# Attention and FFN in two layers on one core: the splitting of the row maxima moves from VectorE to GpSimd, and two projections change places

## What is computed

```python
# layer 0
x = x + attention(tc_rmsnorm(x, t, g1w, g1b, b1w, b1b), Wq, Wk, Wv, Wo)
y = x + (silu(h @ gate_w.T) * (h @ hid_w.T)) @ out_w.T      # h = tc_rmsnorm(x, ...)
# layer 1
attn = softmax(where(mask, -inf, q @ k.T * D ** -0.5))
out = (attn @ v) @ Wo.T
xn = out / sqrt(mean(out * out) + EPS) * rms_scale * (1 + sc) + shift
```

## Time and profile before

| what | value |
|---|---|
| median of 3 runs | 1013.13 us (1012.89 to 1013.67) |
| the profiled execution | 1013.52 us, its span 1011.7 us |
| mean granted TensorE clock | 0.955 |
| busy: PE, DVE, ACT, POOL | 91%, 66%, 51%, 36% of the span |

### The profile page before, as it was taken

One profiled execution on the slowest core, in us unless ns is written; L12 is line 12 of the kernel. 1 busy time (PEld: TensorE's weight loads), 2 busy tenths in 40 slices (PEclk: granted clock), 3 DMA queues, 4 the chain that ended last, 5 costly groups with the idle time before them and its releaser, 6 DMA issues.

```text
span 1011.7 us, 24345 instructions
## 1 busy us (share of the span) xinstructions
PE 916.5 (91%) x8188; PEld 784.3 (78%) x8188; DVE 663.7 (66%) x1424; ACT 515.9 (51%) x1066; POOL 361.8 (36%) x376
## 2 busy tenths in 40 slices
PE   3568899999999999999999999999998888988884
PEld 2446698898888988988889889989886767767663
DVE  3476658667576686675765766656567777878751
ACT  2235546546455455364454554554456655656452
POOL 5322334334343434333334343333433333434221
PEclk9769999999999999999999999999999999999885
DMA  5554422432242233222422242333346575766700
GB/s 177 135 105 106 105 64 60 83 72 56 50 98 48 62 70 76 63 58 58 94 42 63 70 89 65 76 68 73 82 97 147 138 166 134 161 145 147 159 23 23
DMA packets 83070, 91.29 MB, mean 90 GB/s; under 512 B 7776, under 2 KB 70016, under 8 KB 83008
## 3 DMA queue, kind: packets, MB, share of 16 engines
q1 hardware_dynamic: 83008, 90.50, 40.1%
HBM read 60.30 MB, written 29.36 MB: 89 GB/s over the span
## 4 chain that ended last, share of the span: by engine, by line
PE 63%; DVE 16%; issue 7%; DMA 6%; ACT 4%; SPq 2%; POOL 1%; DVEq 0%; ACTq 0%; POOLq 0%
PE work L515 10%; PE work L517 10%; PE work L516 10%; PE s2ps L596 6%; DMA stack<-rows 5%; PE pvps L612 5%; PE s1ps L573 5%; PE work L699 3%; PE work L646 3%; DVE nmax L871 2%; PE acc L515 2%; PE acc L516 2%; PE acc L517 2%; DVE th L967 2%; DVE nrest L889 2%
## 5 line engine op out<-in xcount | busy, mean ns | idle before, releaser
L1067 ACT ACTIVATE E<-s2ps 128x512 f32<-128x512 f32 x384 | 214.0, 596 | 196.6 <-PE s2ps L596 123.7
L871 DVE TENSOR_REDUCE nmax<-s1ps 128x2 f32<-128x512 f32 x256 | 163.9, 682 | 15.8 <-PE s1ps L573 15.1
L515 PE MATMUL work<-xch,Gh 128*128 128x256 f32 x512 | 154.4, 302 | 0.1
L1305 POOL TENSOR_TENSOR hl<-hf,hh 128x256 fp32r<-128x256 f32 x128 | 94.7, 740 | 148.2 <-PE acc L517 93.1
L516 PE MATMUL work<-xcl,Gh 128*128 128x256 f32 x512 | 147.2, 287 | 0.0
L517 PE MATMUL work<-xch,Gl 128*128 128x256 f32 x512 | 147.1, 287 | 0.0
L967 DVE SCALAR_TENSOR_TENSOR th<-th,work 128x256 f32<-128x256 f32 x128 | 53.9, 421 | 136.6 <-ACT th L1085 135.4
L596 PE MATMUL s2ps<-stack 100*128 100x256 bf16 x768 | 128.8, 277 | 9.7 <-DMA stack<-rows 9.4
L515 PEld LDWEIGHTS work<-xch,Gh 128*128 128x128 f32 x512 | 99.5, 194 | 8.4 <-issue 6.6
L612 PE MATMUL pvps<-E,vaug 128*32 128x256 f32 x1536 | 98.7, 391 | 5.9 <-ACT E L1067 3.6
L517 PEld LDWEIGHTS work<-xch,Gl 128*128 128x128 f32 x512 | 100.0, 195 | 0.0
(11 more groups left out here) (130 smaller groups left out, 2192.3 us busy)
## 6 DMA issues: line engine op xcount, KB each, us to landing
stack<-scr SPq DMA_DIRECT2D x64, 384.0 KB, 4.7
stack<-scr SPq DMA_DIRECT2D x64, 256.0 KB, 5.4
scr<-qp SPq DMA_DIRECT2D x64, 192.0 KB, 2.3
scr<-kp SPq DMA_DIRECT2D x64, 192.0 KB, 2.3
stack<-scr SPq DMA_DIRECT2D x64, 128.0 KB, 5.7
X<-xT SPq DMA_DIRECT2D x16, 256.0 KB, 4.7
yT<-crm SPq DMA_DIRECT2D x16, 256.0 KB, 5.5
stack<-rows SPq DMA_DIRECT2D x196, 4.0 KB
```

Source lines behind the costliest of these rows:

```text
L515: mm(out, lh, rh, start=first, stop=False, skip_group_check=True)
L871: v.tensor_reduce(nmax[:, g // 4, qh, 2 * (g % 4):2 * (g % 4) + 2], s1ps[u % 2][:, :].rearrange("p (h t) -> p h t", h=2), AX_X, ALU.max, n ...
L1067: a.activation(E[:, exp_slot(st.L["B2"], st.full, g, kh), :], s2ps[g % 2 if short else u % 2][:, :], ACT.Exp, scale=SCORE_SCALE).then_inc( ...
L1305: p.tensor_tensor(hl[:, i % 2, :], hf[:, i % 2, :], hh[:, i % 2, :].bitcast(F32), ALU.subtract).then_inc(h_low, 1)
```

## The change

GpSimd takes the four small operations of `shift_split`; DVE keeps the clamp, which now stands in slots 3 and 7. There are no copies among them: where DVE cast, GpSimd multiplies by ones. The transposes of the parts come later: half 1 in slot 1 instead of 0, half 0 from step 19 on in slot 5 behind the scores instead of slot 4, with ACT's copy in slot 6 instead of 5. The middle parts of query and key move from DVE to ACT, to the end of the slot. For layer 1, PE does the value projection ahead of the output projection, ACT copies `y` in slot 4 behind `xnh` instead of in slot 3, POOL squares it in slot 5 behind `xnl` instead of in slot 3, and `mean_squares` with what follows it stands in slot 6 instead of 5 (`ms_slot`), ahead of that slot's scores. PE no longer waits for the bank of `T1a` or `T1b` twice.

```diff
+def ms_slot(L):
+    if L["N"] == 0 or L["C"] == 0:
+        return 5
+    return None if L["C"] is None else 6
...
 # bank_uses
-        if g == 0 and L["B2"] is not None:
-            uses.append("sh1")
         if g == 1 and L["C"] is not None:
             uses += ["T1a", "T1b"]
+        if g == 1 and L["B2"] is not None:
+            uses.append("sh1")
...
-        if g == 3 and L["C"] is not None:
+        if g == 3 and L["C"] == 0:
             uses.append("Wo")
...
         if g == 3 and L["V"] is not None:
             uses.append("V")
...
+        if g == 3 and L["C"] == 1:
+            uses.append("Wo")
+        if g == ms_slot(L):
+            uses.append("ms")
...
 # PE
-                        if g == 0:
+                        if g == 1:
                             shift_transpose(st, 1)
...
-                    if g == 4 and L["B1"] is not None and st.s0 >= SPARE:
+                    if g == 5 and L["B1"] is not None and st.s0 >= SPARE:
                         shift_transpose(st, 0)
-                    if g == 3 and L["C"] is not None:
...
+                    if g == 3 and L["C"] == 0:
                         output_projection(st)
...
                         value_projection(st)
+                    if g == 3 and L["C"] == 1:
...
+                        output_projection(st)
...
 # DVE
+            def clamp_maxima(st, half_):
                 nm = nmax[:, half_, :, :]
+                after(dve, s1_free, UNITS * st.n(1) + 8 * half_ + 8)
+                v.tensor_scalar(nm, nm, CLAMP, None, ALU.min).then_inc(shift_clamped, 1)
...
-                b, k = st.bank(use)
-                after(dve, work_free[b], k + 1)
-                v.tensor_copy(parts[:, 1, :, :], rest[:, :, :]).then_inc(mid, 1)
...
 # ACT
+            def middle(st, use, parts, mid):
+                b, k = st.bank(use)
+                after(act, work_free[b], k + 1)
+                a.copy(parts[:, 1, :, :], rest[:, :, :]).then_inc(mid, 1)
...
+                    if g == 6 and st.s0 >= SPARE:
                         if L["B1"] is not None:
                             shift_store(st, 0)
...
-                        if g == 0:
+                        if g == 1:
                             shift_store(st, 1)
...
+                    if g == q_slot(L):
+                        middle(st, "Q", qp, q_mid)
+                    if g == q_slot(L, 1):
+                        middle(st, "K", kp, k_mid)
...
 # POOL
+                p.tensor_tensor(nparts[:, :, 0, :], nm, one, ALU.mult).then_inc(shift_order, 1)
+                after(pool, shift_order, done + 1)
+                p.tensor_tensor(nrest[:, :, :], nm, nparts[:, :, 0, :], ALU.subtract).then_inc(shift_order, 1)
+                after(pool, shift_order, done + 2)
+                p.tensor_tensor(nparts[:, :, 1, :], nrest[:, :, :], one, ALU.mult).then_inc(shift_order, 1)
+                after(pool, shift_order, done + 3)
+                p.tensor_tensor(nparts[:, :, 2, :], nrest[:, :, :], nparts[:, :, 1, :],
+                                ALU.subtract).then_inc(shift_parts, 1)
...
+                    if g == 4 and L["B1"] is not None:
+                        shift_split(st, 0)
                     if g == 4 and L["N"] == 1:
...
+                    if g == (3 if L["C"] == 0 else 5) and L["C"] is not None:
+                        b, k = st.bank("Wo")
...
+                    if g == ms_slot(L):
+                        inverse_roots(st)
...
+                if L["B1"] is not None:
+                    shift_split(st, 1)
```

More of the change, by code:

```diff
@@ L69 @@
 BRANCH = B - 1
-SHIFT_OPS = 4
+SHIFT_OPS = 3
 FIRST, LAST = -3, 2 * B + 1
@@ L915, in o_split, with qk_split @@
                  .then_inc(free, 1)
-            def qk_split(st, use, parts, hi_at, high, mid, low):
+            def qk_split(st, use, parts, hi_at, high):
                 n = st.n(2)
@@ L992, in step @@
                             normalize(st, "bcR", crm[:, :, :], y[:, :, :])
-                    if g == 5 and (L["N"] == 0 or L["C"] is not None):
+                    if g == ms_slot(L):
                         rsqrt(st)
@@ L1157, in step @@
                         affine(st, crm, C_SCALE, C_SHIFT, n - B, c_affine, 2 * (n + 1))
-                    if g == 3 and L["C"] == 1:
-                        bank, free = opened(st, "Wo")
-                        if L["R"] is not None:
-                            b, k = st.bank("bcR")
-                            after(act, work_free[b], k + 1)
-                        else:
-                            act.wait_ge(z_ready, B)
-                        a.copy(flat(y[:, :, :]), bank[:, :]).then_inc(free, 1)
                     if g == 3 and L["V"] is not None:
@@ L1175, in step @@
                                X[:, bass.ds(n - B, 1), :, :].rearrange("p o c t -> p (o c) t")).then_inc(n_hi, 1)
+                    if g == 4 and L["C"] == 1:
+                        bank, free = opened(st, "Wo")
+                        if L["R"] is not None:
+                            b, k = st.bank("bcR")
+                            after(act, work_free[b], k + 1)
+                        else:
+                            act.wait_ge(z_ready, B)
+                        a.copy(flat(y[:, :, :]), bank[:, :]).then_inc(free, 1)
                     if L["C2"] is not None:
@@ L1235, in low_q, with shift_split @@
                                 ALU.subtract).then_inc(low, 1)
+            def shift_split(st, half_):
+                n = st.n(1)
+                k = 2 * n + half_
+                done = SHIFT_OPS * k
+                nm = nmax[:, half_, :, :]
+                one = units[:, :][:, None, :].to_broadcast([P, TC, 8])
+                after(pool, shift_clamped, k + 1)
+                if half_ or st.L["B2"] is not None:
+                    b, k = st.bank("sh0" if half_ else "sh1")
+                    after(pool, work_full[b], k + 1)
+                p.tensor_tensor(nparts[:, :, 0, :], nm, one, ALU.mult).then_inc(shift_order, 1)
[6 more added lines that the diff above has]
+                                ALU.subtract).then_inc(shift_parts, 1)
             def inverse_roots(st):
@@ L1267, in step @@
                         p.tensor_tensor(crm[:, :, :], crm[:, :, :], xb(n - B), ALU.add).then_inc(out_ready, 1)
-                    if g == 3 and L["C"] is not None:
-                        b, k = st.bank("Wo")
-                        after(pool, work_free[b], k + 1)
-                        b, k = st.bank("bcR") if L["R"] is not None else \
-                            st.last().bank("bcN" if st.last().L["N"] == 0 else "bcC")
-                        after(pool, work_full[b], k + 1)
-                        p.tensor_tensor(dg[:, :, :].rearrange("p (c u) t -> p c (u t)", c=FC),
-                                        y[:, :, :], y[:, :, :], ALU.mult).then_inc(sq_c, 1)
+                    if g == 4 and L["B1"] is not None:
+                        shift_split(st, 0)
                     if g == 4 and L["N"] == 1:
@@ L1284, in step @@
                                         xnh[1 - st.par][:, :, :].bitcast(F32), ALU.subtract).then_inc(n_lo, 1)
+                    if g == (3 if L["C"] == 0 else 5) and L["C"] is not None:
+                        b, k = st.bank("Wo")
+                        after(pool, work_free[b], k + 1)
+                        b, k = st.bank("bcR") if L["R"] is not None else \
+                            st.last().bank("bcN" if st.last().L["N"] == 0 else "bcC")
+                        after(pool, work_full[b], k + 1)
+                        p.tensor_tensor(dg[:, :, :].rearrange("p (c u) t -> p c (u t)", c=FC),
+                                        y[:, :, :], y[:, :, :], ALU.mult).then_inc(sq_c, 1)
+                    if g == ms_slot(L):
+                        inverse_roots(st)
                     if g == 5:
-                        if L["N"] == 0 or L["C"] is not None:
-                            inverse_roots(st)
                         if L["C"] == 0:
```

54 lines of the change are left out of this document (17 added, 37 removed).

## The result

The changed kernel took **1042.36 us** (median of 4 runs, 1037.01 to 1047.97) against 1013.01 (4 runs, 1009.05 to 1013.67) for the kernel before in the same comparison: a ratio of **1.0295, 95% interval 1.0258 to 1.0332**. It is slower. The profiled execution is the fastest of the four: 1037.01 us, with a span of 1035.1 against 1011.7 before.

What follows compares the result with a forecast made beforehand. PE's own work was taken to bound layer 0, PE's waits layer 1. Profiled 1013.5 us, +16.5 for steps 18 to 28, +1.2 behind them, -1.5 fill, layer 0 nothing: 1029.7; +3 for clock: 1032, range 1005 to 1046.

Steps and rivals of the forecast that it cites:

- The chain from the key projection to the mean of the squares: Layer 1: from the key projection's end to `mean_squares` 10.35 us, against 7.69 before; PE stands some 2 us there.
- The clock: Layer 1: two falls of PE's granted clock at 1.5 us each, counted as +3 us.
- rival 1: Layer 1: the clock falls in each of 11 steps, 1.5 us more each, 1046 us in all; chance 0.27.
- The rest of the loop: Layer 1: from `mean_squares` back to the next key projection's end, 8.84 us against 9.98 before; whole step 19.2 us.
- Together: Steps 18 to 28: 11 x 1.5 = 16.5 us, plus 3 us for two falls of the clock.
- Rival 2: Layer 1: squares not late, waits for `ol` and the parts saved, 1.0 us a step, 1001 us; chance 0.16.
- Rival 3: Layer 1: the wait for the squares just replaces those for `ol` and the DMA, 1012 to 1015 us; chance 0.07.
- Rival 2's warning: Layer 1: the key's path to the rows' DMA grows by 0.16 us, so much gain would only lengthen that wait.
- `ol` and `oh`: Layer 1: ACT's `oh` starts about 0.9 us later behind the key cast; PE's 0.76 us wait for `ol` nearly goes.
- The fill: Filling of the pipeline: DVE's parts of the maxima hold PE less, -1.5 us, between 0 and -3.
- Layer 0: Layer 0 steps: 0 us change each, between -0.5 and +0.3, staying at 39.6 us.
- The steps behind layer 1's loop: Step 29, without `xnl`, and step 30, without a key: +1.2 us together.

Runs made afterwards that it cites:

- Experiment 2: The changed kernel with 16 unused matmuls added on PE ahead of the wait for the squares in steps 19 to 28: 1025.16 us, ratio 1.0119 to the kernel before.
- experiment 9: The kernel before with three extra, overwritten squarings on GpSimd ahead of the real one in layer 1: 1067.62 us, ratio 1.0509.
- experiment 5: The changed kernel with squares ahead of `xnl`, `y` copied ahead of `xnh`, and the middle parts back on DVE: 1019.35 us, ratio 1.0062 to the kernel before.
- experiment 6: As experiment 5, plus six unused matmuls on PE ahead of the mean of the squares: 1015.36 us, ratio 1.0018 to the kernel before.
- experiment 3: The kernel before with only layer 1's value projection put ahead of the output projection, and ACT's copies in that order: 1023.96 us, ratio 1.0098.
- experiment 10: The kernel before with the split on GpSimd but transposes and ACT's copies in their old slots: 1017.13 us, ratio 1.0027.
- experiment 8: The kernel before with only the middle parts of query and key moved from DVE to ACT: 1021.18 us, ratio 1.0083.
- experiment 7: The kernel before with GpSimd's split, the later transposes and no second wait for the bank of `T1a` or `T1b`: 1009.48 us, ratio 0.995.
- experiment 1: The changed kernel with layer 1's squares ahead of `xnl` and ACT's copy of `y` ahead of `xnh`: 1021.29 us, ratio 1.0075 to the kernel before.
- experiment 4: The changed kernel with the middle parts of query and key back on DVE: 1038.23 us, ratio 1.0245 to the kernel before.

## Why the prediction was right, and where it was not

The forecast was 1032 us in a range of 1005 to 1046, with 0.77 on slower; the median is 1042.4, the profiled execution 1037.0. The sign holds, and so does the half of the mechanism that is the chain: the squares became late and PE stands for them. The other half, the clock, was put down as a side cost and is the larger one. The median lies outside the 1022 to 1038 that was named as this case's own range and is nearer to rival 1's 1046 than to the forecast. Of the sum, two terms were well off and partly made up for each other.

- **The chain from the key projection to the mean of the squares** was forecast at 10.35 us and is 10.39 (887.93, the start of `bcR`, to 898.32). Link by link it is within 0.14 us: ACT's middle part at 0.73 behind the rest, `oh` 0.52 behind it (forecast 0.59), GpSimd's split 1.25 (1.2), `dg` to PE 1.19 (1.05). Twice VectorE's time, 1.6 us for the split, would have been too much. The stand of 2.2 us lies in the 1.5 to 2.5 that were named.
- **The rest of the loop** was put at 8.84 us and is 8.2 (879.72 to 887.93). A third pair of scores with its wait and its gap cost 0.84 in the kernel before (880.79 to 883.32, against 879.72 to 881.41 now), where I had taken 0.64, 0.44 for the pair and 0.2 for the bank; the wait for the rows in that loop was 1.00 (ended 887.53), where I had taken the mean, 0.8; the wait for ACT's last copy is 0.16, where I had taken 0.3. That is 0.54 of the 0.63. So a step at full clock is 18.62 us and not 19.2, below the 18.8 that was named as its least: +0.9 a step, where the forecast had +1.5. That is the term that was too large.
- **The clock** was counted at two falls, +3 us. It fell in 10 of the 11 steps at 1.5 us each (20.13 - 18.62), 15 us: 12 us more than the term. That is the step of the prediction that failed. The rows were read the right way ("resembles step 29 more than any steady step"), and then given too little weight: rival 1 was the right mechanism, at 0.27. Experiment 2 takes the standing away and the falls with it; experiment 9 brings both into the kernel before, with a second stand beside the first. What spoke against it, that waits of 0.8 us never did it, was no argument about 2 us, and those 0.8 us stood elsewhere: for `ol` ahead of a whole projection, and for the rows ahead of scores. The rule on idling between groups of matmuls that the Trainium skill gives (TensorE: Matmul & The Clock Gate, A second HAM failure mode) agrees with this trace, 10 falls in 11 steps. Layer 0's slow steps, which the prediction counted for that rule, show no idling (see behind this list).
- **Together** the 11 steps were forecast at 16.5 + 3 = 19.5 us and cost 25.5: 0.9 x 11 + 1.5 x 10 = 24.9, and the rest is in steps 18 to 20, at 20.2 to 20.4 us.
- **Rivals 2 and 3** fell with the chain of 10.39 us. Rival 2's warning was right, though: in experiments 5 and 6, where the squares come sooner, the wait for the rows by DMA is back at 0.7 and 1.4 us a step.
- **`ol` and `oh`.** `oh` starts 1.92 us behind the key cast (888.13 to 890.05), 1.05 later than before, where 0.9 was named. The wait for `ol` shrank to 0.23 us a step, as forecast, but experiment 3 shows that this was no gain: alone, the new order costs 1%.
- **The fill** was put at -1.5 and gave -4.9. The wait of rows 10 went from 2.7 to 0.8 us, and the 0.8 us for ACT's copy of the rows (L1104) are gone (not in experiment 10, so they belong to the later transposes). Another 1.7 is PE's wait for `cT`, 10.3 us before and 8.6 after; that is no gain of the change, since it is 8.6 or 8.7 in experiments 3, 8 and 9, too, which split on DVE. The other waits moved by up to 1.1 us either way and were not followed. The kernels with the split begin step 1 at 93.8 to 96.0 us, those without it at 96.9 (experiment 8), 97.3 (experiment 9), 98.5 (experiment 3) and 99.6 (before). So the split is worth some 3 us there, and the rest was a late start of the one execution that was profiled before.
- **Layer 0** was put at nothing, and its full steps are 39.6 us as before. The mixed steps 13 to 17 were not costed at all, and cost 2.9 us. The order alone leaves them as they were (175.6 us in experiment 3); the middle parts on ACT add 1.0 (176.6 in experiment 8), the split with its transposes 0.9 (176.5 in experiment 7); a last 1.0 shows only with all parts together. The steps behind layer 1's loop gave 1.2 us, where +1.2 was forecast.

Against the profiled run the errors cancelled in part, by luck: the loop cost 6 us more than forecast, the mixed steps 2.9 and the ramp 0.9, while the fill gave 3.4 more and the end 2.4. The profiled run is also the fastest of the four. The number was better than its reasons.

**Falls without a stand.** In layer 0 of the kernel before PE waits for nothing over 0.1 us in the 9 us ahead of the fall at 268.3, and has just run two groups of eight one-column matmuls:
```profile
265.49 0.95 PE L699 MATMUL work<-mean,nrm 128*128 128x1 f32 x8
266.30 1.03 PE L699 MATMUL work<-mean,dg 128*128 128x1 f32 x8
```
The other four falls there come at the same place of their steps, 0.9 to 1.5 us behind these. So in layer 0 the clock falls behind sixteen one-column matmuls without a stand, in five steps of eleven; in steps 18 to 28 of layer 1, with eight of them, no fall is seen without a stand of 0.4 us or more close by. That the small matmuls and the stand work together is argued from this and not tested, since no run takes the small matmuls away.

What stays open: what decides between a fall in a few steps and in all. Length and place of the stand count, but are not enough: the one step of the changed kernel without a fall has the same stand (2.16 us) as its neighbours. The runs give points, not a bound: 0.2 us close ahead of the one-column matmuls no fall in steps 18 to 28 of the kernel before, yet one in each of its steps 29 and 30, where no projection follows; 0.8 us 3 falls (experiments 1 and 10), but in experiment 5 six, and two more after DMA waits; 1.1 us 9 falls in 10 steps (experiment 3); 2.2 us 10 in 11 (after), 9 in 11 (experiment 4); 1.6 us ahead of a projection 2 in 10 (experiment 8).

## What to carry to other kernels

When an operation changes its engine, list what stands behind it in the new engine's queue and ask who waits for the last of that; here four operations of 0.22 us were cheap, and the squaring put behind them and behind `xnl` was not. A part of a change that is good alone (the split with its transposes, ratio 0.995) can be lost in one that is bad alone (the order, 1.010; the middle parts, 1.008), so each is timed by itself. A stand of TensorE ahead of small matmuls was priced twice here, as time and as clock: what it costs should be read from a step in which both occur. A stand that can't be removed did less harm ahead of a whole projection (experiment 8), or filled with unused matmuls (experiment 2).

## What the runs showed of the hardware that was not expected

A multiplication or subtraction on 128x16 elements takes GpSimd 0.22 us, 0.30 from start to start when each waits for the one before; VectorE undisturbed takes 0.17 and 0.21. VectorE's small operations were thus hardly faster, and next to a GpSimd operation of 128x512 VectorE's cast took 1.25 us and its last subtraction 1.03 (experiment 3), as the cast of the earlier trace rows already showed with 1.26. PE filled with 16 products of 256 columns through a wait of 2.2 us kept the full clock in ten steps of ten, at no cost in time to the step. And with the squares early the load of the stack became a wait of up to 1.9 us (experiments 5 and 6), where it had never held PE in these steps of the kernel before. A fall of the clock costs less where PE would have waited for a DMA anyway (experiment 5).
